# A quantised MLP unrolled in groups of four tiles, and V's projection split around the last rank sums

## The reference

```python
def _weight_quant(w):                       # third layer: quantised MLP
    scale = 1.0 / jnp.clip(jnp.mean(jnp.abs(w)), 1e-05)
    return jnp.clip(jnp.round(w * scale), -1.0, 1.0) / scale
def _act_quant(x):
    scale = 127.0 / jnp.clip(jnp.max(jnp.abs(x), axis=-1, keepdims=True), 1e-05)
    return jnp.clip(jnp.round(x * scale), -128.0, 127.0) / scale
gate = silu(act_quant(x) @ weight_quant(w_gate).T)      # 128 -> 512
up   = act_quant(x) @ weight_quant(w_up).T
return act_quant(gate * up) @ weight_quant(w_down).T    # 512 -> 128
```

```python
def _focus(x, f):                           # fourth layer: cross-attention over 257 context tokens
    x = abs(where(x >= 0, x, 0.01 * x)) + 1e-6
    return softmax(log(x) * f, axis=-1) * x.mean(axis=-1, keepdims=True)
q, k, v = focus(q @ Wq.T), focus(k @ Wk.T), v @ Wv.T    # 16 heads of 8 channels
qh, kh = top5_of_8(qh), top5_of_8(kh)                   # keep the 5 largest of the 8 in each head
y = qh @ (kh.T @ vh / n) / (qh @ mean(kh) + 1e-6)
return y @ Wp.T
```

## Time and profile before

| | us |
|---|---|
| median of three runs | 2837.02 (2836.5 to 2841.46) |
| the profiled execution | 2837.81 |
| its span in the trace | 2835.7 |
| third layer, from 1996.9 to 2113.8 | 116.9 |
| fourth layer, from 2114.7 to 2409.1 | 294.4 |

### The profile page before, as it was taken

How to read it: one execution, slowest core, us unless ns; L and a number is a source line. 1 busy time by engine, 2 the same in 40 slices (tenths; PEclk the granted TensorE clock), 3 DMA queues, 4 the chain that set the end, 5 groups by cost and what they waited for, 6 DMA issues and landing times. The chain is left out here.

```text
span 2835.7 us, 35494 instructions
## 1 busy us (share of the span) xinstructions
PE 2469.1 (87%) x12324; PEld 1394.8 (49%) x12350; DVE 2181.6 (77%) x2846; ACT 1854.4 (65%) x2597; POOL 841.8 (30%) x470
## 2 busy tenths in 40 slices
PE   6799999998799999999999999998446887556997
PEld 3466666663344444444444444443124776354775
DVE  5687777772999999999999999996557776465554
ACT  5465555554799888888889988886425664214443
POOL 0121211111444444444444444443001000301554
PEclk9999999999999999999999999999657999656999
DMA  1000000002000000000000000000000110200221
GB/s 69 12 19 16 17 18 16 15 1 82 0 0 0 38 0 38 0 37 0 38 0 23 14 0 38 0 0 0 12 21 15 37 37 15 94 27 25 76 69 38
DMA packets 26069, 68.11 MB, mean 24 GB/s; under 512 B 3192, under 2 KB 15288, under 8 KB 24632
## 3 DMA queue, kind: packets, MB, share of 16 engines
q1 hardware_dynamic: 25632, 64.13, 6.6%
q10 hardware_dynamic: 288, 2.10, 0.2%
HBM read 60.91 MB, written 5.31 MB: 23 GB/s over the span
## 5 line engine op out<-in xcount | busy, mean ns | idle before, releaser
L251 PE MATMUL a_ps<-a_x,a_w 128*128 128x512 f32 x1536 | 695.9, 598 | 25.8 <-DVE a_kf L599 13.2
L251 PEld LDWEIGHTS a_ps<-a_x,a_w 128*128 128x128 f32 x1536 | 291.6, 191 | 405.5 <-issue 368.0
L774 POOL TENSOR_TENSOR a_den<-a_qf,a_ksum 128x1024 f32<-128x1024 f32 x128 | 271.0, 2117 | 512.4 <-DVE a_qf L592 475.8
L777 POOL TENSOR_TENSOR a_num<-a_qf,a_kvsum 128x1024 f32<-128x1024 f32 x128 | 294.8, 2303 | 185.6 <-DVE a_kvsum L617 185.6
L2425 DVE TENSOR_REDUCE x_rn<-x_sqk 128x8 f32<-128x512 f32 x256 | 174.3, 682 | 106.4 <-ACT x_sqk L2349 102.3
L2349 ACT ACTIVATE x_sqk<-x_b_k 128x512 f32<-128x512 f32 x256 | 153.1, 598 | 157.2 <-PE x_b_k L2261 150.9
L262 PE MATMUL a_ps<-a_att,a_w 128*128 128x512 f32 x480 | 215.8, 592 | 0.0
L592 DVE SCALAR_TENSOR_TENSOR a_qf<-a_eq,a_qf 128x1024 f32<-128x1024 f32 x128 | 195.4, 1527 | 1.7
L2242 POOL TENSOR_TENSOR x_kn<-x_craw,x_w 128x256 f32<-128x256 f32 x64 | 46.9, 734 | 503.8 <-DVE x_craw L2414 482.2
L445 ACT ACTIVATE a_den<-a_den,consts 128x1024 f32<-128x1024 f32 x128 | 147.0, 1149 | 55.9 <-POOL a_den L774 55.9
L599 DVE SCALAR_TENSOR_TENSOR a_kf<-a_ek,a_ps 128x1024 f32<-128x1024 f32 x128 | 155.6, 1215 | 30.2 <-ACT a_ps L441 22.8
(11 more groups left out here) (398 smaller groups left out, 5307.9 us busy)
## 6 DMA issues: line engine op xcount, KB each, us to landing
a_w<-layers SPq DMA_DIRECT2D x8, 2577.0 KB, 9.4
x_craw<-ctx SPq DMA_DIRECT2D x32, 256.0 KB, 2.7
y_cx<-ctx_t SPq DMA_DIRECT2D x16, 512.0 KB, 3.6
m_wb<-m_scratch SPq DMA_DIRECT2D x16, 512.0 KB, 3.8
m_w<-experts SPq DMA_DIRECT2D x8, 544.0 KB, 4.9
x_w<-xattn_w ACTq DMA_DIRECT2D x1, 1536.0 KB, 9.4
x_all<-x_t SPq DMA_DIRECT2D x4, 256.0 KB, 9.3
t_scratch<-t_q_t SPq DMA_DIRECT2D x4, 256.0 KB, 3.7
```

The lines of the kernel that those rows point to most:

```text
L251: last = nc.tensor.matmul(bank(tile, j), col(par, part * HK + u * P, P), x[:, t0:t0 + BANK], start=True, stop=True)
L774: nc.gpsimd.tensor_tensor(by_batch(den[:, b, :]), by_batch(qf[:, b, :]), bcast(ksum[:, b, :], S), ALU.mult).then_inc(d_ready, 1)
L777: nc.gpsimd.tensor_tensor(by_batch(num[:, b, :]), by_batch(qf[:, b, :]), bcast(kvsum[:, b, :], S), ALU.mult).then_inc(n_ready, 1)
```

## The change

**Third layer.** `l0_ffn` no longer calls `layernorm_all`; all is one block, straight-line code without loops. PSUM is used by its eight banks of 512 columns. The square of the layer norm moves from POOL to ACT, and ACT does all four squares ahead of the first logarithm. The sum of the weights stands on DVE between the third and the fourth centring. The product of weights and scale moves to ACT. Quantising is done in four groups of four tiles. In the MLP, Silu, product and maximum of the next group interleave with quantising, turning and down projection of this group; rounding to integer (`to_integer`: add minus ROUND, write bf16) and the scaling of y move from DVE to ACT, so that DVE has two instead of three operations of 512 columns to quantise a tile. The turned hidden tile has one bank (4), so turning tile t waits for the copy of tile t - 1. The turning of y and its addition go by groups too, behind the hidden work of the group after.

The parts of the diff that set the order:

```diff
+                def gate_up(t):
+                    pe.wait_ge(xq_kept, t // per + 1)
+                    wait_past(pe, h_ready, t - 1)
+                    b = 2 * (t % 2)
+                    for i in range(2):
+                        last = nc.tensor.matmul(bank(b + i), xqt[:, t * P:(t + 1) * P], wt[:, i, :], start=True, stop=True)
+                    last.then_inc(gu_ready, 1)
+                def turn_h(t):
+                    pe.wait_ge(h_quant, t + 1)
+                    wait_past(pe, h_kept, t)
...
+                for p in range(parts):            # TensorE
+                    t = per * p
+                    if p == 0:
+                        gate_up(2)
+                        gate_up(3)
+                    if p + 1 < parts:
+                        gate_up(t + 4)
+                        gate_up(t + 5)
...
+                    turn_h(t)
+                    turn_h(t + 1)
+                    down(t)
+                    turn_h(t + 2)
+                    down(t + 1)
+                    turn_h(t + 3)
+                    down(t + 2)
+                    if p + 1 < parts:
+                        gate_up(t + 6)
+                    down(t + 3)
+                    if p + 1 < parts:
+                        gate_up(t + 7)
+                    turn_y(p)
...
+                for p in range(1, parts):         # VectorE
+                    normalise(p)
+                quantise_x(0)
+                round_weights()
+                for p in range(1, parts):
+                    quantise_x(p)
+                hidden(0)
+                hidden(1)
+                add(0)
+                hidden(2)
+                add(1)
+                hidden(3)
+                add(2)
+                add(3)
```

```diff
-                def project_v(m, b):
-
-                    wait_past(pe, v_kept, m - 2)
-                    for t in range(tiles_of(m)):
+                def project_v(m, b, tiles):
+
+                    if tiles[0] == 0:
+                        wait_past(pe, v_kept, m - 2)
+                    for t in range(tiles[0], min(tiles[-1] + 1, tiles_of(m))):
...
                     ranks(n, (1, 2, 3))
                     if not fixed or 2 <= n + 1 <= LAST:
-                        project_v(n + 1, 1 - b)
+                        project_v(n + 1, 1 - b, (0, 1, 2))
                     ranks(n, (4, 5, 6, 7))
+                    if not fixed or 2 <= n + 1 <= LAST:
+                        project_v(n + 1, 1 - b, (3, 4, 5, 6, 7))
...
-                    compare(n, b, (1, 2))
+                    compare(n, b, (1, 2, 3))
                     if not fixed or n < LAST:
                         minus_max(n + 1, 1 - b)
-                    compare(n, b, (3, 4, 5, 6, 7))
+                    compare(n, b, (4, 5, 6, 7))
```

More of the change, by code:

```diff
@@ L809, in l0_ffn @@
[L809 to L810 removed]
+        wr = sb("wr", [P, 3, FF])
         wt = sb("wt", [P, 3, FF], BF16)
[L813 to L819 removed]
@@ L839, in _ @@
             @block.tensor
             def _(pe):
-                for t in range(TILES):
-                    last = nc.tensor.transpose(wide(t // 8)[:, t % 8, :], xn[:, t * P:(t + 1) * P], ident)
-                last.then_inc(x_turned, 1)
-                pe.wait_ge(wsum_done, 1)
-                nc.tensor.matmul(banks[2][:, 0:3], ones, wsum[:, :], start=True, stop=True).then_inc(wsum_read, 1)
-                pe.wait_ge(x_quant, 1)
-                turned = banks[3][:, :].bitcast(BF16).rearrange("p (t c) -> p t c", c=P)
@@ L849, in _, with mean, var @@
-                for t in range(TILES):
-                    last = nc.tensor.transpose(turned[:, t, :], xq[:, t, :], identb[:, :])
-                last.then_inc(xq_turned, 1)
+                def mean(p):
+                    nc.tensor.matmul(bank(p), ones, x_in[:, of(p)], start=True, stop=True).then_inc(mean_ready, 1)
+                def var(p):
+                    pe.wait_ge(squared, p + 1)
+                    nc.tensor.matmul(bank(4 + p), ones, tmp[:, of(p)], start=True, stop=True).then_inc(var_ready, 1)
@@ new lines, in down, with turn_y @@
+                def down(t):
+                    pe.wait_ge(h_kept, t + 1)
+                    wait_past(pe, y_set, t - 1)
+                    for c in range(FCH):
+                        last = nc.tensor.matmul(bank(6 + t % 2)[:, 0:P], hqt[:, t % 2, c * P:(c + 1) * P],
+                                                wt[:, 2, c * P:(c + 1) * P], start=(c == 0), stop=(c == FCH - 1))
+                    last.then_inc(down_done, 1)
+                def turn_y(p):
+                    pe.wait_ge(y_set, per * (p + 1))
+                    wait_past(pe, x_out, p)
+                    for t in range(per):
+                        last = nc.tensor.transpose(bank(5)[:, t * P:(t + 1) * P], y[:, (per * p + t) % (2 * per), :], ident)
+                    last.then_inc(y_turned, 1)
@@ new lines, in _ @@
+                for p in range(parts):
+                    mean(p)
+                for p in range(parts):
+                    var(p)
+                    if p == 2:
+                        pe.wait_ge(w_summed, 1)
+                        pe.wait_ge(centred, 1)
+                        nc.tensor.matmul(bank(0)[:, 0:3], ones, wsum[:, :], start=True, stop=True).then_inc(w_mean, 1)
+                turn_x(0)
+                turn_x(1)
+                turn_x(2)
+                turn_x(3)
+                pe.wait_ge(ident_set, 1)
@@ new lines, in scale_y @@
+                def scale_y(t):
+                    act.wait_ge(down_done, t + 1)
+                    wait_past(act, y_turned, t // per - 1)
+                    nc.scalar.activation(y[:, t % (2 * per), :], bank(6 + t % 2)[:, 0:P], ACT.Copy, scale=hback[:, t:t + 1]).then_inc(y_set, 1)
+                nc.scalar.preload_act_table_set(LOG_EXP)
+                for p in range(parts):
+                    act.wait_ge(centred, p + 1)
+                    nc.scalar.activation(tmp[:, of(p)], xn[:, of(p)], ACT.Square).then_inc(squared, 1)
```

327 lines of the change are left out of this document (182 added, 145 removed).

## The result

The changed kernel takes 2795.57 us (median of 4, 2792.12 to 2799.93) against 2837.71 us (median of 4): a ratio of 0.985, 95% interval 0.9833 to 0.9867. That is 42.1 us less, where I forecast 51. The time lies in the range, 9.6 us above the forecast.

The account below looks back on a forecast made before the run. Bound: a chain round the engines in the third layer, VectorE and TensorE waiting for each other each step in the fourth. Terms -25.6 - 17.3 - 8.1 = -51.0 from 2837.81 give 2786.8, median 2786.0; range 2778 to 2802.

Parts of the forecast that it names:

- Third layer to the first product: Third layer, first centring to first product: VectorE sets the pace, four x groups of 3.75 us; 2.9 us gained.
- Groups: Third layer's four-tile groups: first 10.8 us, then 14.3 each with VectorE waiting 2.0 and 1.5 us for Silus; tail 6.4.
- T + 5.0: Third layer's groups: the Silu of t+6 ends 5.0 us after T, the end of the group's last clip.
- No table load beyond the listed one: Rival, third layer: table loads between Silu and copies, 18 x 1.28 = 23 us, time 2809; chance 0.03.
- groups don't overlap: Rival, third layer: each queue's next instruction waits, a tile costs its whole 7.0 us chain; 2845 us; chance 0.03.
- V's tail: Fourth layer: five of V's tiles move behind the seventh rank sum, covered by select; step 13.07 to 11.87 us, -17.3 in all.
- it has over ten us until it is read: Fourth layer: SP's load goes out 1.1 us later in the step, with over ten us until its reader.
- Unit 3's step: Fourth layer, unit 3's step: gains 0.5 us, its gain less V's tail at the low clock ahead of K.
- the tail falls into that: Fourth layer, unit 2's step: V's tail falls into VectorE's wait for POOL's 14.06 us.
- The slow steps: Fourth layer: five steps of 14.69 us, 1.62 us each, vanish as TensorE idles less; -8.1 us, bounds 0 and -8.1.
- V gives nothing: Rival, fourth layer: splitting V gains nothing because keep_values or the sums' chain paces the step; 2811 us; chance 0.06.
- slow steps stay: Rival, fourth layer: the clock still drops every third step although the gap is shorter; 2794.1 us; chance 0.25.

Follow-up runs that it names:

- e8: Changed kernel with gate and up and the Silus of t+6 and t+7 one place earlier in the third layer's queues; 2792.5 us (0.984).
- e11: Changed kernel with gate and up of t+6 ahead of down t+1, of t+7 ahead of turning t+3, Silus moved up too; 2787.7 us (0.9813).
- e4: Changed kernel with each context load of the fourth layer's loop sent in two pieces; 2786.4 us (0.982).
- e3: Changed kernel with V of unit 3 projected whole in unit 2's step, all other steps split; 2793.8 us (0.9843).
- e5: Changed kernel with V's projection unsplit, eight tiles between the third and fourth rank sum; 2808.6 us (0.9902).
- e9: Kernel before with five unneeded matmuls a step in TensorE's gap ahead of sums in the fourth layer; 2834.8 us (0.9992).
- the fillings: Unneeded matmuls in TensorE's gap: kernel before with five (2834.8 us) or two (2831.8 us); new third layer with old fourth, with five (2805.1 us).
- e2: Kernel before with only the new fourth layer, the third layer as before; 2824.0 us (0.9954).

## Why the prediction was right, and where it was off

The 9.6 us above the forecast are the sum of errors of both signs: the third layer gave 4.1 us more than its term, the fourth 8.3 less in the trace and some 12 less by the medians, and the trace has 5.9 us lost in the fifth and sixth, which I had counted as nothing. That the number fell into the range is in part luck.

- **Third layer to the first product**: forecast 29.1 us from the first centring, measured 26.7. A group of x costs VectorE 3.34 us (2017.64 to 2020.98, start to start) and not 3.75; I had put its seams too high. Four of them are 1.6 of the 2.4 us; ACT's logarithms ended 0.6 earlier for most of the rest.
- **Groups**: first one 10.2 us instead of 10.8, then 13.9, 13.9 and 13.7 instead of 14.3, waits 1.45 to 2.29 and 1.26 instead of 2.0 and 1.5, tail 6.6 instead of 6.4; the last addition ends 85.1 us after the first centring instead of 89. Of the 0.4 to 0.6 us by which a group was forecast too long, 0.15 is a slip of the sum: its terms up to the Silu of t+6 add up to T + 4.85, not T + 5.0. The mechanism was right, and e8 and e11 confirm that the waits came from the queues' order. No table load beyond the listed one: that rival is out, as is "groups don't overlap".
- **V's tail**: right in mechanism. e4 gives 11.90 for the 11.87 of the sum. What failed is the sentence on SP's load, "it has over ten us until it is read". The load fills the buffer that the very next `project_k` reads. The trace of before had it: 5.4 us from issue to reader, of which the load takes 3.6, so 1.8 to spare and not over ten. And against the next `select` the issue moved by 2.3 us, from 0.98 ahead to 1.3 behind, since `select` itself was to come 1.2 us earlier. K was due 4.45 us behind the start of `select` (2238.22 - 2233.77), which leaves 3.1 us for a load of 3.6: an estimate of 0.5 from the rows of before. I had followed VectorE's and ScalarE's queues past the moved tiles, and on SP's only the moment of issue. Price: 0.45 to 0.48 us a step (12.35 against e4's 11.90 and the forecast's 11.87), 6 us in 13 steps.
- **Unit 3's step**: forecast 0.5 us gained, measured 3.9 lost (11.72 to 15.59). The step that failed is "the tail falls into that": it doesn't fall into POOL's time but behind it, since the rank sum ahead of it in the queue waits for just that. e3 removes it.
- **The slow steps**: all gone, as forecast, and with less idle time of TensorE, the reason given: e5 brings them back with the gap, e9 removes them without the split. Their worth for the whole kernel is less sure than the 8.1 us of the fourth layer's trace. An estimate from the medians: the fast steps gave 13 x 0.73 = 9.5 us and unit 3 took 3.9, so of the 12.3 to 13.6 us some 7 to 8 are left for the slow steps here, while the fillings show 1.2 to 5.7.
- **"V gives nothing"** is out by e2 and e5, "slow steps stay" too. The figure of the latter, 2794.1, came nearest to the time, for another reason.
- Outside both layers I had counted nothing; there the traces spread over 8 us.

e4, with the load put right and unit 3's step in part, stands at 2786.4 us, 0.4 from the forecast. That doesn't make the sum right term by term: the third layer's 4.1 us more cover unit 3's step, which still takes 1.4 us more than before where 0.5 less was forecast, and whatever of the slow steps' 8.1 us the whole kernel doesn't show.

## What to carry to other kernels

When work is moved down a queue, follow the signal it gives as well: find the next reader of the buffer that this signal lets be refilled, count from the new issue to that reader, and set this against the time that the load takes, at every place where the moved work can be held up, the odd first step above all. Where two engines wait for each other in turn, move independent work from the side that is late into the other side's gap until one of them is full. Put nothing that others wait for behind an instruction that waits for a single buffer.

## What the hardware showed

- With TensorE idle for 1.64 us ahead of `sums` in each step of 13.1 us, and busy for 154.5 of 178 us in all, the granted clock fell in five of some fourteen steps, to 0.50 (1.2 GHz) from 2250 to 2252 in the step of the earlier trace rows; with 1.1 us idle there it fell in two, with 0.45 in none. The mean clock from 2206 to 2384 was 0.95, 0.98 and 1.00.
- The same instructions of the fifth and sixth layer took 426.1 to 434.5 us in 14 traces. The step from unit 0 to unit 1 took 9.42 us in the trace of before and 10.84 to 11.06 in all others, by TensorE's clock at that moment (transposes and K in 2.9 us at 1.00 there, in 4.5 us at 0.62 in the changed kernel). Single traces of this kernel can't be compared to less than some 5 us outside steps that repeat.
- One comparison of 64x16 took VectorE 14.03 us beside a GpSimd product of 14.12 us.
